# Two matrix products one quarter later in a hand-written order, and three small operations moved from VectorE to ScalarE

## The chip, the cores and the metric

The kernel runs on one core of one Trainium2 chip. The metric is the device time of one execution in microseconds (us). The core's engines are TensorE (PE in the views, PEld for its weight loads), VectorE (DVE), ScalarE (ACT), GpSimd (POOL) and SyncE (SP, which issues DMAs here). They run on their own and meet at semaphores.

## The reference

Sixteen images of 128 channels and 32 x 32 pixels go through three layers (cut to what matters):

```python
# L0: attention over 1024 pixels, 4 heads of 32 channels, per image b
qkv = einsum('oc,bchw->bohw', qkv_w, batchnorm(x)) + qkv_b
attn = softmax(einsum('bnchw,bncyx->bnhwyx', q, k) / sqrt(C))
x = x + out_w @ einsum('bnhwyx,bncyx->bnchw', attn, v) + out_b
# L1: linear attention on t = tokens of x, 8 heads of 16 channels
z = layernorm(t)                      # per token
d = z - mean_of_each_head(z);  u = d / (std_of_each_head(d) + EPS)
k = kln_weight * u + kln_bias;  v = vln_weight * u + vln_bias
t = t + z + z @ (k.T @ v / N)         # per head; k.T @ v comes from u.T @ u
# FFN: 8 experts, the two likeliest of each token
z2 = layernorm(t);  probs = softmax(z2 @ gate_w + gate_b)
t = t + sum over the top 2 experts of probs * (gelu(z2 @ W1 + b1) @ W2 + b2)
```

## The kernel before, in words

One loop of 19 iterations (`FIRST` = -1 to `LAST` = 17) holds a software pipeline over images. In iteration i, TensorE computes the attention of image i, and beside it what comes before and after for its neighbours: q, k, v of image i+1, the first layer norm, `z`, `u` and the Gram product of image i-1, the second layer norm and the gate of image i-2, the expert slots of image i-3. Fourteen images are routed: their tokens are scattered to DRAM by expert and go through the experts in tiles of 256 tokens, from iteration 16 on and after the loop. The last two go through all experts.

An iteration has 32 quarters (q). Each engine walks them in order in its own program, and the tables `AT` (iterations -1 to 15) and `AFTER` (16 and 17) say in which quarter each piece of side work stands. Nothing but semaphores ties the quarters of one engine to those of another. In TensorE's program every even quarter begins with `scores` (L1755, L1758: the scores of one key block, four heads), every odd one with `values` (L1789: probabilities times v); both kinds then have two row tiles (L1814: scores again, by rows, from which VectorE takes the row maxima of the next half image, L1345). Two row tiles have two banks, so a row tile waits until the tile before the last has been reduced. The side products, called pieces, stand between the two row tiles. They all write one PSUM bank (`shared_ps`), so a piece waits until the one before it in the order has been copied out:

```python
def order(pair, p):
    return sorted(LAG, key=lambda n: table(pair, p)[n])   # equal quarters: as in LAG
...
def free_shared(name, pair, p):                           # TensorE, ahead of each piece
    prev_name, prev_pair, prev_p = previous(name, pair, p)
...
    elif prev_name[:4] == "mrow":
        pe.wait_ge(mrow_ready, 2 * b + int(prev_name[4]) + 1)
...
    elif prev_name == "gram":
        pe.wait_ge(gram_out, 3 * b + 2)
```

`LAG` names `mrow0` ahead of `gram` and `usum`.

The pieces that the change is about: **gram** (L1639, 16 passes over `u` of image i-1: u.T @ u and the sum of u), which waits for `u_ready` of GpSimd; **usum** (L1644, the product behind it: it spreads the sum of u over the partitions), which waits for `udiag` that ScalarE makes from gram's result; **mrow0** (L1616: turns the negative row maxima `negm` of image i+1 into a row, which `scores` of the next iteration add), which waits for `negm` of VectorE (`row_maxima`, L1138 to L1147, in q28 behind the first row maximum of that quarter). ScalarE copies gram out (L865 to L869) and mrow0 (L834). In an even quarter its program has a piece between the two exponentials (L928) of that quarter, in an odd one behind them.

`u` is made in a chain over four engines: ScalarE writes `z` (L902); VectorE sums groups of 16 (`gsum`, L1404) and scales the sums to means (L1408); GpSimd subtracts (`d16`, L782); ScalarE squares (L974); VectorE sums the squares (L1412); ScalarE takes logarithm and exponential (L894, L896); VectorE makes the reciprocal deviations (`head_deviations`, up to L1199); GpSimd multiplies (`u`, L787).

For the routed images VectorE also makes slot numbers (`slot_numbers`): it advances the token numbers by 1024 (L1329), sums two products to slot numbers (L1330) and converts these to integers (L1332), which GpSimd's scatter (L715) reads.

Of the kernel before, what the change touches and what calls it, by code (L numbers as in the profile page):

```python
# [10 lines left out]
ALU = mybir.AluOpType  # L11
# [8 lines left out]
def conv_attention_hybrid_kernel(  # L20
# [62 lines left out]
    out_v = out.rearrange("b c h w -> b c (h w)")  # L83


    AT = {'q0': 2, 'k0': 3, 'q1': 4, 'k1': 7, 'rank': 1, 't2_0': 8, 't2_1': 10, 'proj0': 11, 'proj1': 12, 'mrow1': 14, 'v0': 13, 'v1': 16, 'z2T0': 17, 'z2T1': 18, 'logits': 20, 'zT0': 23, 'zT1': 27, 'mrow0': 29, 'gram': 28, 'usum': 30, 'xn': 0, 'values1': 0, 'values0': 17, 'x_bias': 27, 'ln1': 11, 'z2': (12, 14, 14, 15), 'gexp': 21, 'ln0': 16, 'z': (18, 18, 20, 21), 'square': 21, 'ln_heads': 26, 'split': (2, 3, 5, 6), 'norm1': 5, 'norm0': 29, 'd16': (20, 20), 'u': (22, 23), 'scatter': (8, 10, 11, 13, 16, 17, 22, 24), 'max1': 12, 'max0': 28, 'kv1': 2, 'kv2': 4, 'kv3': 5, 'slot_numbers': 4, 'stats1a': 8, 'stats1b': 10, 'deviations1': 11, 'gate': (20, 21, 23, 23, 24, 25, 25, 25, 26, 26, 26, 27, 27, 27, 27, 27), 'prefix': (27, 28, 30), 'stats0a': 11, 'stats0b': 12, 'deviations0': 17, 'gsum': (19, 20), 'ss': (22, 24), 'heads': 26, 'turn': 1, 'den_sum': 2, 'sum': (5, 9, 13, 19), 'den1': 5, 'den0': 21}

    LAG = {
# [3 lines left out]
    }  # L92
    AFTER = (
        {**AT, **{'rank': 0, 't2_0': 10, 't2_1': 10, 'proj0': 10, 'proj1': 12, 'z2T0': 17, 'z2T1': 18, 'logits': 20, 'zT0': 21, 'zT1': 24, 'gram': 28, 'usum': 31, 'values1': 12, 'ln1': 3, 'z2': (12, 13, 14, 14), 'gexp': 19, 'ln0': 15, 'z': (17, 17, 18, 18), 'square': 20, 'ln_heads': 23, 'norm1': 8, 'd16': (19, 20), 'u': (25, 26), 'scatter': (3, 3, 4, 5, 5, 6, 7, 10), 'kv1': 2, 'kv2': 4, 'kv3': 7, 'slot_numbers': 1, 'stats1a': 10, 'stats1b': 10, 'deviations1': 11, 'gate': (23, 23, 24, 24, 25, 25, 26, 27, 27, 28, 28, 29, 29, 29, 29, 30), 'prefix': (26, 28, 29), 'stats0a': 11, 'stats0b': 13, 'deviations0': 16, 'gsum': (18, 19), 'ss': (21, 22), 'heads': 24, 'den1': 3}},
        {**AT, **{'rank': 0, 't2_0': 7, 't2_1': 10, 'proj0': 11, 'proj1': 13, 'z2T0': 17, 'z2T1': 18, 'logits': 20, 'zT0': 21, 'zT1': 23, 'gram': 28, 'usum': 30, 'values1': 4, 'ln1': 11, 'z2': (12, 13, 14, 14), 'gexp': 20, 'ln0': 15, 'z': (17, 17, 18, 18), 'square': 20, 'ln_heads': 23, 'norm1': 5, 'd16': (18, 19), 'u': (25, 26), 'scatter': (0, 0, 2, 5, 8, 11, 14, 17), 'kv1': 0, 'kv2': 4, 'kv3': 6, 'slot_numbers': 0, 'stats1a': 9, 'stats1b': 11, 'deviations1': 11, 'gate': (21, 21, 22, 23, 23, 24, 25, 25, 25, 26, 26, 27, 27, 27, 27, 28), 'prefix': (26, 28, 29), 'stats0a': 11, 'stats0b': 13, 'deviations0': 16, 'gsum': (18, 19), 'ss': (21, 22), 'heads': 24, 'den1': 5}},
    )
    PAIRS, SUM_PARTS = 4, 4
    SUMMED = (0, 1, 2, 3)
# [130 lines left out]
    with ctx:  # L229
# [3 lines left out]
        def sem(name):  # L233
            return ctx.enter_context(nc.semaphore(name))
# [422 lines left out]
        def _(pool):  # L657
# [87 lines left out]
            def iteration(pair, p):  # L745
                at = table(pair, p)
                for q in range(QUARTERS):
                    s, j = divmod(q, 4)
                    for i in SUMMED:
                        for half in (0, 1):  # L750
                            when = 16 * half + at["sum"][i]
                            lag = -(when // QUARTERS)
                            if q == when % QUARTERS and in_range(lag, pair, p):
                                b = image(lag, pair, p)[0]
                                if i in summed_at(2 * b + half):
                                    sum_pair(b, half, i)
                    if in_range(1, pair, p):
                        b, _, par = image(1, pair, p)
                        if q == at["split"][0]:

                            _, prp, parp = image(0, pair, p)
                            if positive(prp + 1):
                                for h in range(NH):
                                    pool.wait_ge(stacked1[parp][h], 16 * STACK1_DMAS * (prp + 1))
                        for c in range(4):
                            if q == at["split"][c]:
                                split(b, par, c)
                    if in_range(-3, pair, p):
                        b, _, par = image(-3, pair, p)
                        for i in range(8):  # L770
                            if q == at["scatter"][i]:
                                scatter(b, par, range(2 * i, 2 * i + 2))
                    if in_range(-1, pair, p):
                        b, _, _ = image(-1, pair, p)
                        if q == at["norm1"]:
                            norm(b, 1)
                        for half in (0, 1):
                            blocks = slice(4 * half, 4 * half + 4)
                            if q == at["d16"][half]:

                                pool.wait_ge(gsum_ready, 4 * b + 2 * half + 2)
                                g.tensor_tensor(grouped(d16[:, blocks, :]), grouped(z[:, blocks, :]),  # L782
                                                wide16(gsum[:, 1, :])[:, blocks], ALU.subtract).then_inc(d_ready, 1)
                            if q == at["u"][half]:

                                pool.wait_ge(rs_step, 5 * b + 5)
                                g.tensor_tensor(grouped(u[:, blocks, 0:C]), grouped(d16[:, blocks, :]),  # L787
                                                wide16(rs16[:, 1, :])[:, blocks], ALU.mult).then_inc(u_ready, 1)
                    if q == at["norm0"] and in_range(0, pair, p):
                        norm(image(0, pair, p)[0], 0)  # L790
                    for t in steps_at(q, pair, p):
                        scatter_y(t - 3)
# [21 lines left out]
        def _(act):  # L814
# [98 lines left out]
            def iteration(pair, p):  # L913
                at = table(pair, p)
                for q in range(QUARTERS):
# [153 lines left out]
        def _(dve):  # L1069
# [256 lines left out]

            def slot_numbers(b, par):
                dve.wait_ge(slot_step, 4 * b + 3)
                v.tensor_scalar(token[:, :], token[:, :], float(N), None, ALU.add).then_inc(token_ready, 1)  # L1329
                v.tensor_reduce(slot_of[:, :, :], slot[:, 1:3, :, :], AX.X, ALU.add).then_inc(slot_step, 1)  # L1330
                dve.wait_ge(slot_step, 4 * b + 4)
                v.tensor_copy(slot_idx[:, par, :], slot_of[:, :, :].rearrange("p c k -> p (c k)")).then_inc(idx_ready, 1)  # L1332

            def iteration(pair, p):
                at = table(pair, p)
                for q in range(QUARTERS):
# [53 lines left out]
                    if in_range(-1, pair, p):  # L1390
# [7 lines left out]
                        for half in (0, 1):  # L1398
                            blocks = slice(4 * half, 4 * half + 4)
                            groups = slice(4 * NG * half, 4 * NG * half + 4 * NG)  # L1400
                            if q == at["gsum"][half]:
# [611 lines left out]
```

## Time and profile before

| what | value |
|---|---|
| runs | 1842.6, 1842.03 and 1848.09 us (median 1842.6) |
| profiled execution | first to last instruction 1848.0 us, which goes with the run of 1848.09 us: about 0.1 us lies around the span |
| TensorE busy | 1707.3 us, 92% of the span |
| VectorE, ScalarE, GpSimd busy | 72%, 62%, 69% |
| mean granted clock of TensorE | 0.964 |

The span has three parts: a start of some 50 us, the image loop to about 1390 us, and expert tiles with the sums and stores to the end. In the loop an iteration takes some 84 us. A granted clock of 1.00 is TensorE at 2.4 GHz, 0.5 is 1.2 GHz; a stretch that holds both shows a value between.

### The profile page before, as it was taken

The numbers are of one execution on the slowest core, as the hardware profiler recorded it, in microseconds if no ns is written. First come the engines' busy times: TensorE is split into PE (matmuls) and PEld (weight loads), VectorE is DVE, ScalarE is ACT, GpSimd is POOL, SyncE is SP. The second block draws the span as 40 slices with busy tenths as digits, with TensorE's granted clock in tenths as the row PEclk, the third lists the DMA queues.
The fourth block names the chain that finished last, engine by engine and source line by source line (L and its number), as shares of the span: only waits on it lengthen the run. The fifth ranks groups of instructions, "written<-read, shape, count | busy, mean of one in ns | idle before, by whom it ended". The sixth has DMA issues, their size and how long they took to land. (4 is left out here: it accounts for less than half of the span.)

```text
span 1848.0 us, 36083 instructions
## 1 busy us (share of the span) xinstructions
PE 1707.3 (92%) x11741; PEld 842.7 (46%) x11741; DVE 1338.6 (72%) x3555; ACT 1140.8 (62%) x2019; POOL 1279.6 (69%) x1165
## 2 busy tenths in 40 slices
PE   5999989999999999999999999999976889999999
PEld 2223333333434333333334343333335778888776
DVE  5567788888878888888878888878755555555474
ACT  2556565666656665666666566656544777777553
POOL 1466747787878778787778787787874767777500
PEclk8899999999999999999999999999997889999998
DMA  2302112130303031230303030312212334454394
GB/s 77 91 13 58 35 47 61 46 90 29 88 19 88 19 92 46 65 85 23 92 27 89 19 89 18 92 37 63 67 58 78 92 95 127 156 173 137 102 288 157
DMA packets 119206, 144.43 MB, mean 78 GB/s; under 512 B 18248, under 2 KB 83044, under 8 KB 119024
## 3 DMA queue, kind: packets, MB, share of 16 engines
q1 hardware_dynamic: 103856, 110.91, 21.4%
q0 software_dynamic: 14784, 31.23, 5.0%
q8 instruction: 97, 1.59, 0.4%
q14 instruction: 85, 0.70, 0.1%
q10 hardware_dynamic: 384, 0.00, 0.0%
HBM read 59.38 MB, written 50.05 MB: 59 GB/s over the span
## 5 line engine op out<-in xcount | busy, mean ns | idle before, releaser
L1345 DVE TENSOR_REDUCE rowmax<-psum 128x1 f32<-128x512 f32 x992 | 652.3, 682 | 210.0 <-PE psum L1814 203.9
L1814 PE MATMUL psum<-arena 128*128 128x512 bf16 x992 | 360.4, 390 | 38.2 <-DVE rowmax L1345 35.7
L928 ACT ACTIVATE arena<-psum 128x1024 f32<-128x1024 f32 x256 | 253.9, 1022 | 161.1 <-PE psum L1758 161.1
L928 ACT ACTIVATE probs<-psum 128x1024 f32<-128x1024 f32 x256 | 253.1, 1020 | 114.5 <-PE psum L1758 114.2
L1755 PE MATMUL psum<-qk 32*128 32x512 f32 x2048 | 293.9, 643 | 10.0 <-ACT probs L928 4.6
L1814 PEld LDWEIGHTS psum<-arena 128*128 128x128 bf16 x992 | 88.5, 99 | 448.0 <-DVE rowmax L1345 333.4
L715 POOL DMA_INDIRECT sorted_scratch<-rows,slot_idx x224 | 220.3, 984 | 96.8 <-issue 51.9
L729 POOL TENSOR_TENSOR probs<-probs 128x512 f32<-128x512 f32 x172 | 218.9, 1273 | 27.2 <-PE psum L1789 16.1
L729 POOL TENSOR_TENSOR arena<-arena 128x512 f32<-128x512 f32 x172 | 218.9, 1272 | 22.0 <-PE psum L1789 10.1
L803 POOL DMA_INDIRECT y_scratch<-xn,d_tile x120 | 116.9, 974 | 57.5 <-issue 28.7
L1865 PE MATMUL psum<-qk 128*128 128x256 f32 x476 | 129.5, 396 | 20.0 <-ACT qk L988 18.9
L803 POOL DMA_INDIRECT y_scratch<-qk,d_tile x118 | 115.0, 974 | 45.9 <-issue 26.0
L706 POOL TENSOR_TENSOR part<-qk,part 128x512 bf16<-128x512 f32 x64 | 74.0, 1157 | 94.3 <-ACT qk L848 90.7
L1789 PE MATMUL psum<-arena,v_sb 128*32 128x512 f32 x1024 | 138.5, 613 | 0.0
L1789 PE MATMUL psum<-probs,v_sb 128*32 128x512 f32 x1024 | 136.4, 605 | 0.0
L1755 PEld LDWEIGHTS psum<-qk 32*128 32x128 f32 x2048 | 80.5, 183 | 120.5 <-issue 78.3
L1882 PEld LDWEIGHTS psum<-arena,x_in 128*128 128x128 f32 x952 | 128.0, 198 | 13.8 <-issue 7.5
L1882 PE MATMUL psum<-arena,x_in 128*128 x952 | 130.9, 282 | 3.1 <-ACT x_in L1000 3.1
L1000 ACT ACTIVATE x_in<-psum,b_tile 128x256 f32<-128x256 f32 x238 | 100.0, 472 | 38.4 <-issue 31.8
L729 POOL TENSOR_TENSOR arena<-arena,probs 128x512 f32<-128x512 f32 x80 | 102.1, 1277 | 12.9 <-PE psum L1789 7.6
L729 POOL TENSOR_TENSOR probs<-probs,arena 128x512 f32<-128x512 f32 x80 | 102.0, 1275 | 5.5
L1758 PE MATMUL psum<-mrow,ones_b 2*128 2x512 bf16 x1024 | 102.0, 378 | 0.0
(256 smaller groups left out, 2876.5 us busy)
## 6 DMA issues: line engine op xcount, KB each, us to landing
arena<-part SPq DMA_DIRECT2D x256, 128.0 KB, 3.1
part<-sorted_scratch SPq DMA_DIRECT2D x119, 144.0 KB
x_in<-in_x_dram SPq DMA_DIRECT2D x16, 512.0 KB, 3.2
x_res<-in_x_dram SPq DMA_DIRECT2D x16, 512.0 KB, 5.7
t_scratch<-t SPq DMA_DIRECT2D x14, 512.0 KB, 6.4
arena<-t_scratch SPq DMA_DIRECT2D x10, 512.0 KB
probs<-y_scratch SPq DMA_DIRECT2D x16, 256.0 KB, 4.2
out_dram<-v_sb SPq DMA_DIRECT2D x16, 256.0 KB, 3.9
```

Source lines behind the costliest of these rows:

```text
L715: g.indirect_dma_start(out=sorted_dram, out_offset=bass.IndirectOffsetOnAxis(ap=slot_idx[:, par, n:n + 1], axis=0), in_=rows[:, par, n % B ...
L729: piece = g.tensor_tensor(even[:, cols], even[:, cols], odd[:, cols], ALU.add)
L803: g.indirect_dma_start(out=y_dram, out_offset=bass.IndirectOffsetOnAxis(ap=d_tile[:, i, k:k + 1], axis=0), in_=y_out[i][:, k, :], in_offse ...
L928: a.activation(group[:, 2 * i:2 * i + 2, :].rearrange("p s n -> p (s n)"), st_pair[i], ACT.Exp, scale=float(C) ** -0.5).then_inc(exp_done, 1)
L1000: a.activation(hid[t % 2][:, j, :], bank[t % 2][:, j * TILE:(j + 1) * TILE], ACT.Gelu, bias=b1_tile[:, t % 2, j:j + 1]).then_inc(hid_ready, 1)
L1345: v.tensor_reduce(rowmax[:, half, kh, h, j:j + 1], row_ps[kh][:, :], AX.X, ALU.max)\
L1755: t_.matmul(st_ps[h], qk[rows_, par, 1, keys], qk[rows_, par, 0, queries], start=True, stop=False)
L1758: last = t_.matmul(st_ps[h], ones_b[rows_, :], mrow[rows_, half, :], start=False, stop=True)
L1789: mm = t_.matmul(av_ps[rows_, :], v_sb[:, par, kb, rows_], group[:, h, :], start=(kb == 0), stop=(kb == NKB - 1))
L1814: t_.matmul(ps[:, :], qs1[:, par, h, qb * P:(qb + 1) * P], ks1[:, par, h, kh * HALF:(kh + 1) * HALF], start=True, stop=True)\
L1865: last = t_.matmul(bank[t % 2][:, j * TILE:(j + 1) * TILE], w1_tile[t % 2][:, j * P:(j + 1) * P], zT_tile[t % 2], start=True, stop=True)
L1882: last = t_.matmul(bank[4 + t % 2][:, k * P:(k + 1) * P], hid[t % 2][:, j, k * P:(k + 1) * P], w2[:, bass.ds(e, 1), j, :].rearrange("p a c ...
```

## The change

Four edits. (1) In `AT`, gram stands in q29 in place of q28 and usum in q31 in place of q30; the tables `AFTER` keep theirs. mrow0 stays in q29, and at equal quarters `LAG` puts it ahead, so it now comes before gram. (2) The scaling of the group sums moves from VectorE to ScalarE, as an activation (Copy with a scale) with a place of its own, `gmean`, in q19 and q21; GpSimd's `d16` waits for it. (3) The conversion of the slot numbers and (4) the advance of the token numbers move to ScalarE (`slot_indices`, in the quarter of `slot_numbers`, behind a wait for VectorE's sum). VectorE's next slot sum waits until ScalarE has read the last one.

```diff
-    AT = {... 'mrow0': 29, 'gram': 28, 'usum': 30, ... 'gsum': (19, 20), ...}
+    AT = {... 'mrow0': 29, 'gram': 29, 'usum': 31, ... 'gsum': (19, 20), 'gmean': (19, 21), ...}
...
 # GpSimd, iteration
                             if q == at["d16"][half]:
-                                pool.wait_ge(gsum_ready, 4 * b + 2 * half + 2)
+                                pool.wait_ge(gmean_ready, 2 * b + half + 1)
...
 # ScalarE, iteration
+                        for half in (0, 1):
+                            groups = slice(4 * NG * half, 4 * NG * half + 4 * NG)
+                            if q == at["gmean"][half]:
+                                act.wait_ge(gsum_ready, 2 * b + half + 1)
+                                a.activation(gsum[:, 1, groups], gsum[:, 0, groups], ACT.Copy, scale=1.0 / G16)\
+                                 .then_inc(gmean_ready, 1)
...
+                    if q == at["slot_numbers"] and in_range(-3, pair, p):
+                        b, _, par = image(-3, pair, p)
+                        slot_indices(b, par)
...
+            def slot_indices(b, par):
+                act.wait_ge(slot_step, 4 * b + 4)
+                a.activation(slot_idx[:, par, :], slot_of[:, :, :].rearrange("p c k -> p (c k)"), ACT.Copy)\
+                 .then_inc(idx_ready, 1)
+                a.activation(token[:, :], token[:, :], ACT.Copy, bias=float(N)).then_inc(token_ready, 1)
...
 # VectorE
             def slot_numbers(b, par):
                 dve.wait_ge(slot_step, 4 * b + 3)
-                v.tensor_scalar(token[:, :], token[:, :], float(N), None, ALU.add).then_inc(token_ready, 1)
+                if positive(b):
+                    dve.wait_ge(idx_ready, b)
                 v.tensor_reduce(slot_of[:, :, :], slot[:, 1:3, :, :], AX.X, ALU.add).then_inc(slot_step, 1)
-                dve.wait_ge(slot_step, 4 * b + 4)
-                v.tensor_copy(slot_idx[:, par, :], slot_of[:, :, :].rearrange("p c k -> p (c k)")).then_inc(idx_ready, 1)
...
-                                dve.wait_ge(gsum_ready, 4 * b + 2 * half + 1)
-                                v.tensor_scalar(gsum[:, 1, groups], gsum[:, 0, groups], 1.0 / G16, None, ALU.mult)\
-                                 .then_inc(gsum_ready, 1)
```

TensorE's program in q28 to q30 of iteration 14 before, from the first row tile of q28 to the scores of q30, with the semaphores that each row waits for (L1639 is gram, L1616 mrow0):

```order
L1814 MATMUL psum<-arena 128x512 [waits row_used]
L1639 MATMUL psum<-u 128x129 [waits zT_ready,u_ready]
L1639 MATMUL psum<-u 128x129 x7
L1814 MATMUL psum<-arena 128x512 [waits row_used]
L1789 MATMUL psum<-arena,v_sb 32x512 [waits exp_done]
L1789 MATMUL psum<-arena,v_sb 32x512 x3
L1814 MATMUL psum<-arena 128x512 [waits row_used]
L1616 MATMUL psum<-identb,negm 128x128 [waits gram_out,negm_ready]
L1616 MATMUL psum<-identb,negm 128x128 x3
L1814 MATMUL psum<-arena 128x512 [waits row_used]
L1755 MATMUL psum<-qk 128x512 [waits exp_done]
```

The same stretch of the changed kernel, whose lines are numbered 14 higher there (L1653 is gram, L1630 mrow0):

```order
L1828 MATMUL psum<-arena 128x512 [waits row_used] x2
L1803 MATMUL psum<-arena,v_sb 32x512 [waits exp_done]
L1803 MATMUL psum<-arena,v_sb 32x512 x3
L1828 MATMUL psum<-arena 128x512 [waits row_used]
L1630 MATMUL psum<-identb,negm 128x128 [waits zT_ready,negm_ready]
L1630 MATMUL psum<-identb,negm 128x128 x3
L1653 MATMUL psum<-u 128x129 [waits mrow_ready,u_ready]
L1653 MATMUL psum<-u 128x129 x7
L1828 MATMUL psum<-arena 128x512 [waits row_used]
L1769 MATMUL psum<-qk 128x512 [waits exp_done]
```

Gram has moved behind the values, a row tile and mrow0, and directly behind mrow0; in place of `zT_ready` it waits for `mrow_ready`, ScalarE's copy of mrow0, and mrow0 no longer waits for `gram_out`.

ScalarE's program in q27 to q30 of iteration 11 before, from the biasing of the residual in q27 on (L928 are exponentials, L865 to L869 copy gram out, L834 mrow0):

```order
L949 ACTIVATE x_res<-x_res,bo 128x1024
L928 ACTIVATE probs<-psum 128x1024
L865 ACTIVATE usum_sb<-psum 128x1
L866 ACTIVATE kvw<-psum,kcol 128x128
L868 ACTIVATE udiag<-ident,usum_sb 128x128
L869 ACTIVATE kcc<-usum_sb,kb_n,kcol 128x1
L928 ACTIVATE probs<-psum 128x1024
L834 ACTIVATE mrow<-psum 128x512
```

And in the changed kernel:

```order
L950 ACTIVATE x_res<-x_res,bo 128x1024
L929 ACTIVATE probs<-psum 128x1024 x2
L835 ACTIVATE mrow<-psum 128x512
L866 ACTIVATE usum_sb<-psum 128x1
L867 ACTIVATE kvw<-psum,kcol 128x128
L869 ACTIVATE udiag<-ident,usum_sb 128x128
L870 ACTIVATE kcc<-usum_sb,kb_n,kcol 128x1
```

Both exponentials of q28 now stand ahead of gram's copies, and mrow0's copy ahead of them too.

## Rows read from the trace of the kernel before

**Rows 1.** The page's first part: busy us, share of the span, instructions.

```profile
PE 1707.3 (92%) x11741; PEld 842.7 (46%) x11741; DVE 1338.6 (72%) x3555; ACT 1140.8 (62%) x2019; POOL 1279.6 (69%) x1165
```

**Rows 2.** Waits of TensorE, whole span: us in total, times, longest.

```profile
PE psum L1814 <- DVE rowmax L1345: 35.7, 69, 1.7
PE psum L1639 <- POOL u L787: 20.3, 15, 2.8
```

**Rows 3.** Windows, gram (L1639) alone, two of 14: stretch, length, PE busy, granted clock.

```profile
1036.50:1040.30 3.80, 3.33 (x16) 0.62 0.12 39
1121.00:1124.50 3.50, 2.05 (x16) 1.00 0.13 42
```

**Rows 4.** Timeline of TensorE, iteration 12: start, length, what, [idle before <-releaser].

```profile
1119.71 0.39 PE L1814 MATMUL psum<-arena 128*128 128x512 bf16 x1 [0.86 <-DVE rowmax L1345]
1121.34 2.05 PE L1639 MATMUL psum<-u 128*128 128x129 f32 x16 [1.24 <-POOL u L787]
1123.23 0.38 PE L1814 MATMUL psum<-arena 128*128 128x512 bf16 x1
1123.54 1.06 PE L1789 MATMUL psum<-arena,v_sb 128*32 128x512 f32 x8
...
1124.77 0.39 PE L1616 MATMUL psum<-identb,negm 128*128 128x128 bf16 x4
...
1125.39 1.14 PE L1755 MATMUL psum<-qk 32*128 32x512 f32 x8
```

**Rows 5.** Timeline of VectorE in the same stretch.

```profile
1119.02 1.22 DVE L1345 TENSOR_REDUCE rowmax<-psum 128x1 f32<-128x512 f32 x2
...
1122.02 0.68 DVE L1345 TENSOR_REDUCE rowmax<-psum 128x1 f32<-128x512 f32 x1
...
1123.05 0.23 DVE L1147 SCALAR_TENSOR_TENSOR negm<-rowm,negm 128x16 bf16<-128x16 f32 x1
```

**Rows 6.** Timelines of GpSimd and of ScalarE in the same stretch.

```profile
1119.19 2.09 POOL L787 TENSOR_TENSOR u<-d,rs 128x512 f32<-128x512 f32 x2 [4.67 <-DVE rs L1199]
...
1125.22 0.60 ACT L834 ACTIVATE mrow<-psum 128x512 bf16<-128x512 f32 x1
```

**Rows 7.** Timeline of TensorE, iteration 11: row tile of q28, scores of q30.

```profile
1035.21 0.39 PE L1814 MATMUL psum<-arena 128*128 128x512 bf16 x1 [0.86 <-DVE rowmax L1345]
...
1042.39 1.14 PE L1755 MATMUL psum<-qk 32*128 32x512 f32 x8
```

**Rows 8.** Groups of VectorE and ScalarE (busy us, mean ns), and L1408's min/median/max.

```profile
L1408 DVE TENSOR_SCALAR gsum<-gsum 128x32 f32<-128x32 f32 x32 | 31.7, 990 | 1.1
L1332 DVE CAST slot_idx<-slot_of 128x16 uint32<-128x16 f32 x14 | 15.0, 1070 | 0.5
L896 ACT ACTIVATE ss<-ss 128x64 f32<-128x64 f32 x16 | 4.1, 256 | 0.5
L1408 DVE TENSOR_SCALAR gsum<-gsum x32: 181/853/1728, 170.6 to 1424.3; 128x32 f32<-128x32 f32 x32
```

**Rows 9.** Timelines of VectorE, ScalarE and TensorE in iterations 10 and 11.

```profile
890.36 0.69 DVE L1345 TENSOR_REDUCE rowmax<-psum 128x1 f32<-128x512 f32 x1 [0.72 <-PE psum L1814]
...
1022.28 0.69 DVE L1345 TENSOR_REDUCE rowmax<-psum 128x1 f32<-128x512 f32 x1 [1.42 <-PE psum L1814]
...
1013.06 1.94 ACT L928 ACTIVATE probs<-psum 128x1024 f32<-128x1024 f32 x2
1021.70 1.06 ACT L974 ACTIVATE u<-d 128x1024 f32<-128x1024 f32 x1 [3.75 <-POOL d L782]
...
1020.56 1.14 PE L1755 MATMUL psum<-qk 32*128 32x512 f32 x8
```

**Rows 10.** Timeline of TensorE at the end of the last attention (iteration 15) and behind.

```profile
1368.56 3.64 PE L1639 MATMUL psum<-u 128*128 128x129 f32 x16 [2.82 <-POOL u L787]
...
1374.19 1.14 PE L1755 MATMUL psum<-qk 32*128 32x512 f32 x8 [1.00 <-ACT probs L928]
...
1376.90 0.43 PE L1664 MATMUL psum<-chosen,tri 128*128 128x64 f32 x2
```

More of the change, by code:

```diff
@@ L83, in conv_attention_hybrid_kernel @@
     out_v = out.rearrange("b c h w -> b c (h w)")
-    AT = {'q0': 2, 'k0': 3, 'q1': 4, 'k1': 7, 'rank': 1, 't2_0': 8, 't2_1': 10, 'proj0': 11, 'proj1': 12, 'mrow1': 14, 'v0': 13, 'v1': 16, 'z2T0': 17, 'z2T1': 18, 'logits': 20, 'zT0': 23, 'zT1': 27, 'mrow0': 29, 'gram': 28, 'usum': 30, 'xn': 0, 'values1': 0, 'values0': 17, 'x_bias': 27, 'ln1': 11, 'z2': (12, 14, 14, 15), 'gexp': 21, 'ln0': 16, 'z': (18, 18, 20, 21), 'square': 21, 'ln_heads': 26, 'split': (2, 3, 5, 6), 'norm1': 5, 'norm0': 29, 'd16': (20, 20), 'u': (22, 23), 'scatter': (8, 10, 11, 13, 16, 17, 22, 24), 'max1': 12, 'max0': 28, 'kv1': 2, 'kv2': 4, 'kv3': 5, 'slot_numbers': 4, 'stats1a': 8, 'stats1b': 10, 'deviations1': 11, 'gate': (20, 21, 23, 23, 24, 25, 25, 25, 26, 26, 26, 27, 27, 27, 27, 27), 'prefix': (27, 28, 30), 'stats0a': 11, 'stats0b': 12, 'deviations0': 17, 'gsum': (19, 20), 'ss': (22, 24), 'heads': 26, 'turn': 1, 'den_sum': 2, 'sum': (5, 9, 13, 19), 'den1': 5, 'den0': 21}
+    AT = {'q0': 2, 'k0': 3, 'q1': 4, 'k1': 7, 'rank': 1, 't2_0': 8, 't2_1': 10, 'proj0': 11, 'proj1': 12, 'mrow1': 14, 'v0': 13, 'v1': 16, 'z2T0': 17, 'z2T1': 18, 'logits': 20, 'zT0': 23, 'zT1': 27, 'mrow0': 29, 'gram': 29, 'usum': 31, 'xn': 0, 'values1': 0, 'values0': 17, 'x_bias': 27, 'ln1': 11, 'z2': (12, 14, 14, 15), 'gexp': 21, 'ln0': 16, 'z': (18, 18, 20, 21), 'square': 21, 'ln_heads': 26, 'split': (2, 3, 5, 6), 'norm1': 5, 'norm0': 29, 'd16': (20, 20), 'u': (22, 23), 'scatter': (8, 10, 11, 13, 16, 17, 22, 24), 'max1': 12, 'max0': 28, 'kv1': 2, 'kv2': 4, 'kv3': 5, 'slot_numbers': 4, 'stats1a': 8, 'stats1b': 10, 'deviations1': 11, 'gate': (20, 21, 23, 23, 24, 25, 25, 25, 26, 26, 26, 27, 27, 27, 27, 27), 'prefix': (27, 28, 30), 'stats0a': 11, 'stats0b': 12, 'deviations0': 17, 'gsum': (19, 20), 'gmean': (19, 21), 'ss': (22, 24), 'heads': 26, 'turn': 1, 'den_sum': 2, 'sum': (5, 9, 13, 19), 'den1': 5, 'den0': 21}
     LAG = {
@@ L93, in conv_attention_hybrid_kernel @@
     AFTER = (
-        {**AT, **{'rank': 0, 't2_0': 10, 't2_1': 10, 'proj0': 10, 'proj1': 12, 'z2T0': 17, 'z2T1': 18, 'logits': 20, 'zT0': 21, 'zT1': 24, 'gram': 28, 'usum': 31, 'values1': 12, 'ln1': 3, 'z2': (12, 13, 14, 14), 'gexp': 19, 'ln0': 15, 'z': (17, 17, 18, 18), 'square': 20, 'ln_heads': 23, 'norm1': 8, 'd16': (19, 20), 'u': (25, 26), 'scatter': (3, 3, 4, 5, 5, 6, 7, 10), 'kv1': 2, 'kv2': 4, 'kv3': 7, 'slot_numbers': 1, 'stats1a': 10, 'stats1b': 10, 'deviations1': 11, 'gate': (23, 23, 24, 24, 25, 25, 26, 27, 27, 28, 28, 29, 29, 29, 29, 30), 'prefix': (26, 28, 29), 'stats0a': 11, 'stats0b': 13, 'deviations0': 16, 'gsum': (18, 19), 'ss': (21, 22), 'heads': 24, 'den1': 3}},
@@ L95, in conv_attention_hybrid_kernel @@
-        {**AT, **{'rank': 0, 't2_0': 7, 't2_1': 10, 'proj0': 11, 'proj1': 13, 'z2T0': 17, 'z2T1': 18, 'logits': 20, 'zT0': 21, 'zT1': 23, 'gram': 28, 'usum': 30, 'values1': 4, 'ln1': 11, 'z2': (12, 13, 14, 14), 'gexp': 20, 'ln0': 15, 'z': (17, 17, 18, 18), 'square': 20, 'ln_heads': 23, 'norm1': 5, 'd16': (18, 19), 'u': (25, 26), 'scatter': (0, 0, 2, 5, 8, 11, 14, 17), 'kv1': 0, 'kv2': 4, 'kv3': 6, 'slot_numbers': 0, 'stats1a': 9, 'stats1b': 11, 'deviations1': 11, 'gate': (21, 21, 22, 23, 23, 24, 25, 25, 25, 26, 26, 27, 27, 27, 27, 28), 'prefix': (26, 28, 29), 'stats0a': 11, 'stats0b': 13, 'deviations0': 16, 'gsum': (18, 19), 'ss': (21, 22), 'heads': 24, 'den1': 5}},
+        {**AT, **{'rank': 0, 't2_0': 10, 't2_1': 10, 'proj0': 10, 'proj1': 12, 'z2T0': 17, 'z2T1': 18, 'logits': 20, 'zT0': 21, 'zT1': 24, 'gram': 28, 'usum': 31, 'values1': 12, 'ln1': 3, 'z2': (12, 13, 14, 14), 'gexp': 19, 'ln0': 15, 'z': (17, 17, 18, 18), 'square': 20, 'ln_heads': 23, 'norm1': 8, 'd16': (19, 20), 'u': (25, 26), 'scatter': (3, 3, 4, 5, 5, 6, 7, 10), 'kv1': 2, 'kv2': 4, 'kv3': 7, 'slot_numbers': 1, 'stats1a': 10, 'stats1b': 10, 'deviations1': 11, 'gate': (23, 23, 24, 24, 25, 25, 26, 27, 27, 28, 28, 29, 29, 29, 29, 30), 'prefix': (26, 28, 29), 'stats0a': 11, 'stats0b': 13, 'deviations0': 16, 'gsum': (18, 19), 'gmean': (18, 19), 'ss': (21, 22), 'heads': 24, 'den1': 3}},
@@ new lines, in conv_attention_hybrid_kernel @@
+        {**AT, **{'rank': 0, 't2_0': 7, 't2_1': 10, 'proj0': 11, 'proj1': 13, 'z2T0': 17, 'z2T1': 18, 'logits': 20, 'zT0': 21, 'zT1': 23, 'gram': 28, 'usum': 30, 'values1': 4, 'ln1': 11, 'z2': (12, 13, 14, 14), 'gexp': 20, 'ln0': 15, 'z': (17, 17, 18, 18), 'square': 20, 'ln_heads': 23, 'norm1': 5, 'd16': (18, 19), 'u': (25, 26), 'scatter': (0, 0, 2, 5, 8, 11, 14, 17), 'kv1': 0, 'kv2': 4, 'kv3': 6, 'slot_numbers': 0, 'stats1a': 9, 'stats1b': 11, 'deviations1': 11, 'gate': (21, 21, 22, 23, 23, 24, 25, 25, 25, 26, 26, 27, 27, 27, 27, 28), 'prefix': (26, 28, 29), 'stats0a': 11, 'stats0b': 13, 'deviations0': 16, 'gsum': (18, 19), 'gmean': (18, 19), 'ss': (21, 22), 'heads': 24, 'den1': 5}},
```

1 line of the change is left out of this document (added).

## Prediction

> **What bounds the kernel now.** I read the page's first part: TensorE is busy for 92% of the span, the others for 61 to 73% [rows 1]. So the order of work in TensorE's program sets the end, and a change is worth what it adds to or takes from TensorE's waits, plus what the clock does. Then the waits of TensorE [rows 2]. Two of them touch the change: row tiles wait for VectorE's row maxima 69 times, 35.7 us in all, and gram waits for GpSimd's u 15 times, 20.3 us in all. That u-wait is what a later gram could win back, so I looked at gram alone, iteration by iteration [rows 3]. In the fourteen iterations that also hold mrow0 it took 2.05 us at a granted clock of 1.00 (four of them) or 3.0 to 3.7 us with the clock at half for part of it (ten of them). Last, the timelines of TensorE, VectorE, GpSimd and ScalarE in the same stretch of iteration 12, one of the four at full clock [rows 4 to 6]: there the whole change can be replayed.
>
> What happens there now: the first row tile of q28 runs at 1119.71. Gram is next. GpSimd ends u at 1121.28 (1119.19 + 2.09), gram starts 0.06 later, at 1121.34, and runs for 2.05. Row tile (1123.23), values (1123.54), a row tile, mrow0 (1124.77), scores of q30 (1125.39). Meanwhile VectorE, busy with the gate's small steps after 1120.24, takes the row maximum of q28 from 1122.02 to 1122.70 and ends negm at 1123.28 (1123.05 + 0.23) [rows 5]. mrow0 needs that negm and waits for it nowhere, because gram fills TensorE's time until then.
>
> **Gram and usum a quarter later.** I replay the new order with the same rows. u and negm keep their times, since both hang on VectorE's work ahead, which the move leaves as it is. A start lags its releaser by 0.06, as gram's does.
> - The second row tile of q28 needs the reduction that ends at 1120.24 (1119.02 + 1.22): it starts at 1120.30 in place of 1123.23.
> - The values follow by 0.31 (1123.54 − 1123.23): 1120.61, ending near 1121.7.
> - The row tile of q29 needs the bank that VectorE's row maximum frees at 1122.70: 1122.76. A new wait of about 1.1.
> - mrow0 needs negm at 1123.28: 1123.34, and takes 0.39: 1123.73. In front of it TensorE has only that one row tile.
> - Gram stands directly behind mrow0 and uses the same bank, so it waits for ScalarE's copy: 0.06 + 0.60 [rows 6], 1124.39. Gram starts at 1124.45. u has been there since 1121.28.
> - Row tile 1.89 behind gram's start (1123.23 − 1121.34): 1126.34. Scores of q30 0.31 later: 1126.65.
>
> Before, these scores ran at 1125.39: **+1.26 us for each of 14 iterations, +17.6 us.** The u-wait of 1.24 is gone, but two waits that gram covered, for VectorE (1.1 and 0.2) and for ScalarE's copy (0.7), now lie open, because gram is moved behind the one step that it hid. Behind the waiting gram stand the second row tile of q29 and the scores of q30; behind ScalarE's wait for mrow0 stand gram's copies and the exponentials of q30, whose scores come later anyway. usum stands two quarters behind gram as before, so it adds nothing. Lower bound: were neither VectorE's bank nor negm late, mrow0 would start 1.23 behind the values (1124.77 − 1123.54), at 1121.84, its copy would end at 1122.89 and gram start at 1122.95; with the 2.20 from gram to the scores, 1125.15: −0.24, or −3.4 us in 14. I take the replay, as each of its steps is a row.
>
> **The clock.** In iteration 11 gram ran at 0.62 [rows 3], and from q28's first row tile to the scores it was 7.18 us (1035.21 to 1042.39) against 5.68 in iteration 12 (1119.71 to 1125.39) [rows 4, 7]: a fall costs 1.5 us. Each came with a wait of TensorE ahead (0.86 and then the one for u). After the change TensorE idles some 3.1 us in this stretch (0.9, 0.2, 1.1, 0.2 and 0.7), against 2.1 before (0.9 and 1.2), but in smaller pieces between which it works. No row shows what that does. Bounds: none falls, 10 × 1.5 = −15.0; all fourteen fall, 4 × 1.5 = +6.0. I take the same ten of fourteen, 0: more idle time speaks for more falls, its shorter pieces for fewer.
>
> **The end of attention.** Iteration 15 has gram but no mrow0 [rows 10]. Before, gram waits 2.82 for u, and the scores of the last quarter wait a further 1.00 for exponentials that stand behind gram's copies on ScalarE. After, values run in the 2.82 and the second half of the exponentials goes ahead of the copies: scores right behind gram, near 1372.2 (1368.56 + 3.64) instead of 1374.19. That is 2.0 at most, and 0 if usum's wait for the copies takes it back; I take **−1.5**.
>
> **Three operations from VectorE to ScalarE.** VectorE loses 31.7 us of scaling and 15.0 us of conversion [rows 8], and 14 adds no longer than the conversions' 1.07. But right behind both places it waits for TensorE: 0.72 in q4 (890.36) and 1.42 in q20 (1022.28) [rows 9]. What it saves ends in those waits, and the replay's stretch is not moved. ScalarE gains 32 scalings and 28 slot operations, at some 0.26 us each (an activation of 128x64 takes 256 ns). It idles 3.75 ahead of the square [rows 9], which is the chain that the scaling belongs to. The one price: the exponentials of q20 wait behind the scaling for VectorE's sum, by up to 1.0; those ahead end at 1015.00 and the scores of q22 come at 1020.56, so 5.5 us cover it. Without that cover each would cost up to 1.0, 14 us in all. Below, at most what the first rival gives. I take 0.
>
> Here the trace has something to weigh. The scaling of one and the same shape took 181 ns at least and 1728 at most [rows 8]: VectorE is being held up by something. The Trainium skill ("SBUF — State Buffer", section "SBUF: two separate sides") has VectorE and GpSimd share one pair of ports, locked for a whole instruction, and ScalarE on its own; the spread agrees, and by that rule the move takes these hold-ups off VectorE, which is the first rival below.
>
> **Sum.** +17.6 − 1.5 + 0 + 0 = +16.1. The profiled execution takes 1848.1 and would take 1864.2; it is 5.5 above the median of the runs, and the median goes from 1842.6 to **1858.7**.
>
> **Rivals.**
> - *VectorE's freed time reaches the row tiles* (the other side). The 31.7 + 15.0 us and the hold-ups leave VectorE; the 35.7 us that row tiles wait for it vanish: +16.1 − 35.7 = −19.6, 1823.0. For it: mean 990 ns against 181 at least. Against: VectorE waits for TensorE behind each place. It decides once more than 16.1 / 35.7 = 45% of those waits go. Chance 0.10.
> - *The waits vanish and nothing takes their place.* If negm came as early as u, the wait for u (1.24 × 14 = 17.4), the falls (15.0) and the 1.5 would go: −33.9, 1808.7. Against: negm's end at 1123.28 is worked out from a row [rows 5]. Chance 0.05.
> - *The falls vanish.* The idle time is cut in pieces and the clock holds: 16.1 − 15.0 = +1.1, 1843.7, no change. For: iteration 12 kept its clock through waits of 0.86 and 1.24. Chance 0.15.
> - *All fourteen fall.* 16.1 + 6.0 = +22.1, 1864.7. Chance 0.08.
> - *ScalarE's new waits hold the scores*, as with no cover above: 16.1 + 14 = +30.1, 1872.7. Chance 0.04.
>
> **How the numbers follow.** My forecast has 0.58. A change of this kernel can be told from none from about 0.3%, 5.5 us. Faster: 0.10 + 0.05 = 0.15. Same: 0.15. Slower: 0.58 + 0.08 + 0.04 = 0.70. The range goes from 1838 (the lower bound of the move, −3.4 − 1.5, which also takes in the case without falls) to 1867 (all fall, and 2 above it, for what the bounds of the end of attention leave); outside lie the two faster rivals and the last, 0.19. The forecast's own range, with three falls more or less, is 1854 to 1863.
>
> **What would show it.** Right: gram's idle time is put down to ScalarE's mrow in place of GpSimd's u, near 0.7 each; the first row tile of q29 waits about 1.1 for VectorE; at full clock the scores of q30 come some 6.9 us after q28's first row tile (5.7 before); VectorE's busy time falls by 47 us or more, and its waits for TensorE rise by as much. Wrong: row tiles elsewhere wait clearly less than 35.7 us in all (first rival); gram at 1.00 in nearly all iterations (third) or in none (fourth); scores of q22 that wait for exponentials (fifth); mrow0 that doesn't wait for negm, if VectorE got to it sooner than replayed.

## The result, and the profile after

The changed kernel takes 1868.0 us (median of 4 runs, 1861.8 to 1871.6) where the kernel before takes 1843.6: ratio 1.0116, 95% interval 1.0088 to 1.0145. Run again later beside 13 runs of the kernel before it took 1865.6, ratio 1.0105 (1.0083 to 1.0127). By these ratios (the first is not the quotient of its two medians, which would be 1.0132) it is slower by 19 to 21 us; +16.1 was forecast. The first median lies 1.0 above the end of the range, 1867; the second lies within it, as do both ratios applied to the forecast's 1842.6 (1862 to 1864). The profiled execution's span went from 1848.0 to 1867.2 us, by 19.2.

The page's first part, busy us and share of the span by engine:

```profile
PE 1709.5 (92%) x11741; PEld 841.6 (45%) x11741; DVE 1287.5 (69%) x3495; ACT 1148.1 (61%) x2079; POOL 1279.9 (69%) x1165
```

VectorE (DVE) is 51 us less busy than before [rows 1], ScalarE only 7 us more, and TensorE's busy time has grown by 2 us: some 17 of the 19 us are idle time of TensorE. Its waits (total, times, longest), to be read against [rows 2]:

```profile
PE psum L1828 <- DVE rowmax L1362: 54.3, 92, 3.1
...
PE psum L1653 <- ACT mrow L835: 10.9, 14, 0.8
...
PE psum L1630 <- DVE negm L1164: 5.7, 14, 2.0
...
PE psum L1653 <- POOL u L788: 1.8, 1, 1.8
```

The wait for GpSimd's u is gone but for 1.8 of its 20.3 us: the change did what it says. In its place stand 18.6 us more of row tiles that wait for row maxima, 10.9 us of gram waiting for ScalarE's copy of mrow0, and 5.7 us of mrow0 waiting for negm. Where that happens is seen in TensorE's timeline of iteration 10, one of the four that keep the clock up (start, length, what, [idle before <-releaser]); it answers to [rows 4]:

```profile
968.07 0.39 PE L1828 MATMUL psum<-arena 128*128 128x512 bf16 x1 [0.85 <-DVE rowmax L1362]
968.67 0.39 PE L1828 MATMUL psum<-arena 128*128 128x512 bf16 x1 [0.20 <-DVE rowmax L1362]
968.99 1.07 PE L1803 MATMUL psum<-arena,v_sb 128*32 128x512 f32 x8
971.12 0.39 PE L1828 MATMUL psum<-arena 128*128 128x512 bf16 x1 [1.07 <-DVE rowmax L1362]
971.70 0.40 PE L1630 MATMUL psum<-identb,negm 128*128 128x128 bf16 x4 [0.19 <-DVE negm L1164]
972.88 2.02 PE L1653 MATMUL psum<-u 128*128 128x129 f32 x16 [0.78 <-ACT mrow L835]
...
975.05 1.14 PE L1769 MATMUL psum<-qk 32*128 32x512 f32 x8
```

From the first row tile to the scores it is 6.98 us (975.05 − 968.07), against 5.68 in [rows 4]. VectorE in the same stretch works at the times that [rows 5] gave, only moved with the iteration: its row maximum of q28 comes 2.99 behind the pair, negm 4.02 behind it (3.00 and 4.03 before).

```profile
967.39 1.22 DVE L1362 TENSOR_REDUCE rowmax<-psum 128x1 f32<-128x512 f32 x2
...
970.38 0.68 DVE L1362 TENSOR_REDUCE rowmax<-psum 128x1 f32<-128x512 f32 x1
...
971.41 0.23 DVE L1164 SCALAR_TENSOR_TENSOR negm<-rowm,negm 128x16 bf16<-128x16 f32 x1
```

Gram alone, in windows (stretch, length, PE busy, PEld busy, granted clock), iterations 9 and 10 of the fourteen that hold mrow0; ten lie below 1.00 and four at it, as many as before [rows 3]:

```profile
884.90:888.70 3.80, 3.65 (x16) 3.38 (x16) 0.55 0.02 7
972.80:975.00 2.20, 2.02 (x16) 1.86 (x16) 1.00 0.05 12
```

Iteration 2 cost more than any other. TensorE first, then VectorE, then GpSimd, there:

```profile
281.83 0.61 PE L1828 MATMUL psum<-arena 128*128 128x512 bf16 x1 [3.08 <-DVE rowmax L1362]
283.80 0.61 PE L1630 MATMUL psum<-identb,negm 128*128 128x128 bf16 x4 [1.36 <-DVE negm L1164]
```

```profile
278.51 1.19 DVE L1306 TENSOR_TENSOR chosen<-lg 128x64 f32<-128x64 f32 x1
279.74 1.30 DVE L1308 TENSOR_TENSOR rows<-lg,chosen 128x64 f32<-128x64 f32 x1
...
281.10 0.68 DVE L1362 TENSOR_REDUCE rowmax<-psum 128x1 f32<-128x512 f32 x1
```

```profile
276.32 2.07 POOL L788 TENSOR_TENSOR u<-d,rs 128x512 f32<-128x512 f32 x2 [10.12 <-DVE rs L1216]
278.35 10.68 POOL L730 TENSOR_TENSOR probs<-probs,arena 128x512 f32<-128x512 f32 x8
```

`chosen` and `rows` are two of the gate's small steps ahead of q28's row maximum. They take 1.19 and 1.30 here and 0.29 and 0.22 in iteration 10. In iteration 2 no image is routed yet, so GpSimd has no scatters behind u and begins its sums of probabilities at once; in iteration 10 two scatters stand between. So the row maximum and negm come later, the two waits sum to 4.4 us in place of 1.3, and nothing covers them.

In iteration 1 there is no gate yet, and the steps that make negm meet the sums themselves: mrow0 waits 2.02 for negm. VectorE there:

```profile
191.27 1.21 DVE L1162 TENSOR_SCALAR negm<-rowm 128x16 bf16<-128x16 f32 x1
192.52 1.33 DVE L1164 SCALAR_TENSOR_TENSOR negm<-rowm,negm 128x16 bf16<-128x16 f32 x1
```

In iteration 10 these two take 0.20 and 0.23.

The end of attention, which answers to [rows 10]:

```profile
1392.16 2.05 PE L1653 MATMUL psum<-u 128*128 128x129 f32 x16 [1.82 <-POOL u L788]
1394.14 1.14 PE L1769 MATMUL psum<-qk 32*128 32x512 f32 x8
...
1397.45 0.41 PE L1678 MATMUL psum<-chosen,tri 128*128 128x64 f32 x2 [0.54 <-DVE kvw L1250]
```

The values run ahead of gram, the scores follow it with no wait for exponentials, and rank comes 5.29 us behind gram's start (8.34 before). Of these 3.05 us, 1.6 is gram at full clock (2.05 against 3.64), so 1.5 is the order.

### The profile page after: what moved, and what is told of

It is laid out like the page before. It is cut to its first block and busy times, and to the rows that moved or that the text cites. A ratio compares the mean times of both kernels' runs of the same rounds, so it can differ in the third digit from the quotient of the medians.

```text
span 1867.2 us, 36096 instructions
## 1 busy us (share of the span) xinstructions
PE 1709.5 (92%) x11741; PEld 841.6 (45%) x11741; DVE 1287.5 (69%) x3495; ACT 1148.1 (61%) x2079; POOL 1279.9 (69%) x1165
## 5 line engine op out<-in xcount | busy, mean ns | idle before, releaser
L730 POOL TENSOR_TENSOR probs<-probs 128x512 f32<-128x512 f32 x172 | 219.1, 1274 | 27.3 <-PE psum L1803 16.1
```

What stands on the lines that cost most here:

```text
L730: piece = g.tensor_tensor(even[:, cols], even[:, cols], odd[:, cols], ALU.add)
```

## The experiments

Two theories stood first. Lost cover: gram hid TensorE's wait for negm, and behind mrow0 it hides nothing. Rival: the three operations on ScalarE, or its longer queue, cost the time. All ratios are to the kernel before on the same chip, with 95% intervals. Edits are in `AT` unless said.

**Gram and usum alone**, on the kernel before.

```diff
-'gram': 28, 'usum': 30
+'gram': 29, 'usum': 31
```

> The kernel before with gram in q29 and usum in q31 alone; the three small operations stay on VectorE. Lost cover (gram filled TensorE's time until negm, and now stands behind negm's product and its copy): nearly the whole loss is here, +17 to +26 us, ratio 1.009 to 1.014, with gram's wait put down to ScalarE's copy of mrow0 (0.8 each) and the first row tile of q29 waiting 1.1 for VectorE. Rival, that ScalarE's new waits or its longer queue cost the time: under +5 us here, ratio below 1.003.

1863.2 us, 1.0091 (1.0075 to 1.0106), with the wait for ScalarE's copy as large as in the changed kernel (its waits of TensorE):

```profile
PE psum L1639 <- ACT mrow L834: 10.9, 14, 0.8
```

The loss is at the lower end of what lost cover expected (some 17 us), and far above the rival's 5. The move is the loss.

**The three operations alone**: the changed kernel with gram back in q28 and usum in q30.

```diff
-'gram': 29, 'usum': 31
+'gram': 28, 'usum': 30
```

> The changed kernel with gram back in q28 and usum in q30, so only the three small operations have moved. Lost cover: no difference, ratio 0.997 to 1.003, while VectorE is busy some 50 us less and waits as much longer for TensorE. Rival, ScalarE's new waits: +15 us or more, ratio 1.008 and up. Second rival, that VectorE's freed time reaches the row tiles: their 35.7 us of waits shrink and the ratio is below 0.995.

1846.7 us, 1.0001 (0.9988 to 1.0014). VectorE is busy 1282.2 us, 56 less than before, and nothing comes of it; ScalarE's instructions take 13.4 us for what took VectorE 56 (the 31.7 and 15.0 of [rows 8], and 9.3 for the advance). The groups, busy us and mean ns:

```profile
L977 ACT ACTIVATE gsum<-gsum 128x32 f32<-128x32 f32 x32 | 7.3, 229 | 23.7 <-DVE gsum L1421 23.7
L993 ACT ACTIVATE slot_idx<-slot_of 128x16 uint32<-128x16 f32 x14 | 3.1, 223 | 1.9 <-DVE slot_of L1349 1.9
L995 ACT ACTIVATE token<-token 128x8 f32<-128x8 f32 x14 | 3.0, 212 | 0.0
```

Both the ScalarE rival and the first rival of the prediction fall.

**The changed kernel once more**, unaltered.

> The changed kernel once more, beside the others on one chip. If the move of gram and usum is all of its loss, it agrees with the kernel that has that move alone: ratio to before 1.008 to 1.011. Rival, that the three operations on ScalarE add to it once gram stands late: 1.012 or more.

1.0105 (1.0083 to 1.0127), which holds the 1.0091 of the move alone. The two parts add up; the 0.0014 between them, some 3 us, lies within the intervals, so a cost of a few us for the three operations beside a late gram is not excluded.

**An early negm**: the changed kernel, with the gate's last five steps and the first two prefix steps one quarter later.

```diff
-'gate': (..., 27, 27, 27, 27, 27), 'prefix': (27, 28, 30)
+'gate': (..., 28, 28, 28, 28, 28), 'prefix': (28, 29, 30)
```

> The changed kernel with the gate's last five steps and the prefix steps one quarter later on VectorE, so that the row maximum and negm of q28 come some 1.5 us earlier. Lost cover through a late negm: the waits of q29's row tile (1.1 in iteration 12) and of mrow0 go, gram starts about 1.1 earlier, the scores of q30 come 0.1 before those of the kernel before; ratio to before 0.996 to 1.001, and iteration 2 loses its extra 4 us. Rival, that ScalarE's copy ahead of gram or the clock's falls are the cost: gram still waits 0.8 for the copy, the loss stays above +11 us, ratio 1.006 and up.

1839.3 us, 0.9964 (0.9952 to 0.9976). TensorE in iteration 12, and one line of iteration 2:

```profile
1114.36 0.39 PE L1828 MATMUL psum<-arena 128*128 128x512 bf16 x1 [0.85 <-DVE rowmax L1362]
1114.95 0.39 PE L1828 MATMUL psum<-arena 128*128 128x512 bf16 x1 [0.20 <-DVE rowmax L1362]
...
1116.27 0.39 PE L1828 MATMUL psum<-arena 128*128 128x512 bf16 x1
1116.51 0.40 PE L1630 MATMUL psum<-identb,negm 128*128 128x128 bf16 x4
1117.68 2.02 PE L1653 MATMUL psum<-u 128*128 128x129 f32 x16 [0.78 <-ACT mrow L835]
1119.86 1.14 PE L1769 MATMUL psum<-qk 32*128 32x512 f32 x8
```

```profile
280.92 0.40 PE L1630 MATMUL psum<-identb,negm 128*128 128x128 bf16 x4 [2.02 <-DVE negm L1164]
```

In iterations 3 to 14 the waits of 1.07 and 0.19 are gone, the wait for the copy stands, and the scores come 5.50 behind the first row tile (5.68 before, 6.98 in the changed kernel), all at full clock. So the late negm was the loss there, as lost cover has it, and the rival (the copy) isn't. In iterations 1 and 2 mrow0 still waits 2.02 for negm, whose steps meet GpSimd's sums: from q28's scores to the next iteration the two take 7.4 us more than before (9.1 in the changed kernel), so the expectation that iteration 2 loses its extra 4 us held only in part. That the whole became faster than the kernel before comes mostly from the clock: gram's clock fell in 2 of the 14 iterations, these two, not in 10.

**Gram first**: the changed kernel with mrow0 behind gram, and the kernel before with the same order (gram in q29, usum in q31, mrow0 in q30), its three operations left on VectorE.

```diff
-'mrow0': 29
+'mrow0': 30
```

> The changed kernel with mrow0 in q30, so gram comes first in q29; VectorE's gate steps stay where they were. Lost cover: gram again fills the time until negm, with nothing of ScalarE's in front of it; row tile of q29 still waits 1.1, gram starts near 1.73 after the values' end, scores of q30 within 0.15 of the kernel before, mrow0 costs 0.25 more in q30: ratio 0.996 to 1.002, lower by 0.008 if the clock stays up. Rival, that gram in q29 is itself too late: 1.006 or more, as in the changed kernel.

> The kernel before with gram in q29, usum in q31 and mrow0 in q30; the three operations stay on VectorE and the gate's steps where they were. If ScalarE's part is worth nothing, as with gram first and ScalarE's operations: ratio 0.992 to 0.996, with no clock fall at gram and the full-clock length of the stretch as before. Rival, that it takes VectorE's freed time as well: 0.998 or more.

0.9938 (0.9918 to 0.9958) and 0.9929 (0.9908 to 0.9950). The second, TensorE in iteration 12, and its granted clock over the stretch (the number behind the busy times):

```profile
1108.48 0.39 PE L1814 MATMUL psum<-arena 128*128 128x512 bf16 x1 [0.85 <-DVE rowmax L1345]
1109.07 0.39 PE L1814 MATMUL psum<-arena 128*128 128x512 bf16 x1 [0.20 <-DVE rowmax L1345]
...
1111.53 0.39 PE L1814 MATMUL psum<-arena 128*128 128x512 bf16 x1 [1.07 <-DVE rowmax L1345]
1111.76 1.95 PE L1639 MATMUL psum<-u 128*128 128x129 f32 x16
...
1113.85 1.14 PE L1755 MATMUL psum<-qk 32*128 32x512 f32 x8
```

```profile
1105.00:1120.00 15.00, 12.79 (x98) 5.57 (x98) 13.99 (x33) 8.51 (x15) 11.16 (x10) 1.00 0.04 11
```

Gram again fills the time until negm and itself waits for nothing. At full clock nothing is won by the start of the next iteration: the scores of q30 come 5.37 behind the row tile (0.31 earlier than before), and q30 then holds mrow0 and is 0.38 longer. The gain is the clock, which falls near gram in one iteration (the second, where a row tile waits 3.08 for VectorE) instead of ten, and the end of attention.

**Late gate with gram in q28**: the kernel before with the three operations on ScalarE, and the gate edit above.

> The kernel before with the three operations on ScalarE and the gate's last five steps and prefix one quarter later, gram still in q28. Lost cover: an early negm is worth nothing here, since gram waits for u as before (20 us in all) and covers negm anyway; clock falls as before; ratio 0.998 to 1.002. Rival, that the gate's place alone makes the gain of the kernel with the late gate: ratio 0.990 to 0.997.

1905.4 us, 1.0315 (1.0293 to 1.0336): 58 us more than before, where neither theory had a loss above 4. VectorE and GpSimd in iteration 14:

```profile
1344.19 0.69 DVE L1362 TENSOR_REDUCE rowmax<-psum 128x1 f32<-128x512 f32 x1 [1.83 <-PE psum L1828]
1344.79 0.88 DVE L1300 TENSOR_TENSOR lg<-lg,rank_w 128x64 f32<-128x64 f32 x1
1345.71 0.22 DVE L1302 TENSOR_REDUCE lred<-lg 128x8 f32<-128x64 f32 x1
1345.96 1.05 DVE L1304 TENSOR_TENSOR lg<-lg,lred 128x64 f32<-128x64 f32 x1
1347.04 1.31 DVE L1306 TENSOR_TENSOR chosen<-lg 128x64 f32<-128x64 f32 x1
1348.39 1.31 DVE L1308 TENSOR_TENSOR rows<-lg,chosen 128x64 f32<-128x64 f32 x1
```

```profile
1343.30 0.97 POOL L716 DMA_INDIRECT sorted_scratch<-rows,slot_idx  x1 [0.30 <-issue]
1344.28 10.73 POOL L730 TENSOR_TENSOR probs<-probs,arena 128x512 f32<-128x512 f32 x8
```

With gram in q28, the second row tile of q28 comes only behind it, VectorE waits 1.83 for that tile, and its steps then fall beside GpSimd's sums: those with two inputs in SBUF take 0.9 to 1.3 us, the reduction with one stays at 0.22. A row tile of q30 waits 3.2 for them, and TensorE's clock falls behind that wait (the values of q31 take 1.93 us, 1.06 at full clock). It is the mechanism of iteration 2, now in iterations 2 to 14: from the scores of q30 to the next iteration each takes 8.2 to 8.4 us in place of 3.6.

**Late gate and gram first**, on the changed kernel and on the kernel before.

> The changed kernel with mrow0 behind gram (q30) and the gate's last five steps and prefix one quarter later. Lost cover: nothing stands between the values and gram but a row tile whose bank is free; u has been there for 0.7 us. Scores of q30 some 0.9 earlier than in the kernel before: 14 times 0.9 and the gain at the end of attention, -13 to -17 us, ratio about 0.992; if the clock no longer falls in these pieces, 10 times 1.5 more, ratio 0.983. Rival, that VectorE is merely late elsewhere: its delayed gate steps hold the row tiles of q29 and q30, and the ratio is 0.998 to 1.004.

> The kernel before with gram in q29, mrow0 in q30, usum in q31 and the late gate, the three operations on VectorE. If ScalarE's part is worth nothing even where VectorE is busy to the end of the stretch: 0.992 to 0.996, as with ScalarE's operations. Rival, that VectorE without its freed time comes later to the late gate steps: 0.998 or more.

0.9938 (0.9920 to 0.9955) and 0.9935 (0.9914 to 0.9957): no better than gram first alone, and the same with and without ScalarE's three operations. Gram ran at full clock in all fourteen iterations of both, and for that case the first expectation had 0.983: it missed by some 20 us. VectorE and TensorE in iteration 12 of the first:

```profile
1111.41 1.81 DVE L1308 TENSOR_TENSOR rows<-lg,chosen 128x64 f32<-128x64 f32 x1
```

```profile
1114.01 0.39 PE L1828 MATMUL psum<-arena 128*128 128x512 bf16 x1 [0.59 <-DVE rowmax L1362]
```

The scores of q30 come 1.46 earlier than before at full clock, but q30 and q31 then take 4.62 us in place of 3.58: mrow0 stands there, and a row tile waits 0.59 for row maxima behind `rows`, which takes 1.81 beside the sums. Iteration 2 takes over 3 us more than before. What is left against gram first, 0.47 in most iterations, is too little for the intervals.

**Where the steps land**: the late gate with gram first, its last five steps spread further, or three more of them moved, or only `rows` moved.

```diff
 # spread
-'gate': (..., 26, 26, 26, 27, 27, 27, 27, 27), 'prefix': (27, 28, 30)
+'gate': (..., 26, 26, 26, 28, 28, 29, 29, 31), 'prefix': (29, 30, 30)
 # three more
+'gate': (..., 28, 28, 28, 29, 29, 30, 30, 31), 'prefix': (30, 31, 31)
 # only rows
+'gate': (..., 26, 26, 26, 28, 28, 28, 28, 31), 'prefix': (28, 29, 30)
```

> As the kernel with gram first and a late gate, but its last five steps spread over q28, q29 and q31, so that VectorE's longest small step (1.8 us for the rows beside GpSimd's sums) no longer stands before the row maxima of q29. The row tile of q30 there waited 0.6: that goes, 14 times 0.6 = 8 us, ratio to before 0.988 to 0.991. Rival, that the next row tile waits in its place: ratio 0.993 to 0.995, unchanged against that kernel.

> As the kernel with the spread gate, with three more steps moved behind the row maxima of q28 and the rest a quarter further on. The first row tile of q28 waits 0.9 for VectorE in the kernel before and gram's u hangs on the same queue: 0.7 us of steps taken from ahead of it, 14 times up to 0.7 = 10 us, ratio 0.983 to 0.988. Rival, that rank at the start of the next iteration now waits for the late prefix: ratio 0.990 or more, with a wait of rank for VectorE.

> As gram first with the late gate, but the gate's last step (rows, 1.8 us beside GpSimd's sums, 0.2 to 0.3 beside its scatters) alone in q31. If VectorE's small steps are slow only beside GpSimd's sums, the wait of 0.6 at the row tile of q30 goes: ratio 0.987 to 0.991. Rival, that another small step meets the sums in its place (four_of or before, or rows itself in q31): 0.993 to 1.000.

1.0011 (0.9998 to 1.0024), 1.0087 (1.0066 to 1.0108) and 0.9945 (0.9924 to 0.9967). All three expectations failed: the first two took a step to cost the same wherever it stands, and in the third its rival came true (with `rows` gone, `two_of` takes 1.80 in its place, and the row tile of q30 still waits 0.45). `chosen` (min/median/max ns over its 16) in the changed kernel and in the spread one:

```profile
L1306 DVE TENSOR_TENSOR chosen<-lg x16: 225/298/1190, 278.5 to 1561.9; 128x64 f32<-128x64 f32 x16
```

```profile
L1306 DVE TENSOR_TENSOR chosen<-lg x16: 224/1302/1306, 283.0 to 1542.3; 128x64 f32<-128x64 f32 x16
```

In the spread kernel TensorE then waits for row maxima in q31, ahead of usum (L1658), up to 1.6 us and twelve times:

```profile
PE psum L1658 <- DVE rowmax L1362: 19.3, 12, 1.6
```

With three more steps moved the first row tile of the next iteration waits 1.9 for row maxima behind the gate's leftovers, and the clock falls there. Moving `rows` alone gave no gain that its interval tells from gram first.

## Why the prediction was right

- **What bounds, and where.** TensorE's order in q28 to q30 and VectorE's negm, as read. The replay gave idle times of 0.9, 0.2, 1.1, 0.2 and 0.7 in the stretch; measured were 0.85, 0.20, 1.07, 0.19 and 0.78, with the releasers forecast.
- **+1.26 for each of 14.** At equal clock the stretch is 1.30 longer in iteration 10 than in [rows 4]. From q28's scores to the next iteration, iterations 3 to 14 together take 14.3 us more (15.1 forecast; the clock fell near gram in eight of them, in nine before). The term was mis-sized in iterations 1 and 2, where 2.5 was forecast and 9.1 measured (3.54 and 5.51; 5.5 of it more idle time, the rest the clock): I took iteration 12 for all fourteen, though the first two have no scatters on GpSimd that keep its sums away from VectorE's small steps. Before, gram hid that too, but for 0.4 in iteration 2.
- **The clock.** I took ten falls of fourteen, and ten there were. No row stood behind that choice, and the count came out by luck: iteration 1 fell that had not, one fewer of iterations 3 to 14 did, and in iteration 2 gram ran at 1.2 GHz from end to end (3.78 us), more than a fall of 1.5 covers.
- **The end of attention.** −1.5 forecast; −3.0 measured to rank (−3.7 to the scores of q30), half of it a fall that did not come. So the order is worth the 1.5, and the fall was not foreseen.
- **The three operations.** 0 forecast; ratio 1.0001 alone. VectorE lost 51 to 56 us of work, and its freed time ended in waits: in the kernel with the three operations alone its row maxima wait 207.4 us for row tiles and 37.3 more whose releaser the trace doesn't name, against 203.9 before. The 14 us named as the price without cover count fourteen iterations, while the scaling stands in the fifteen from 1 to 15; only the last rival's time hangs on it.
- **The sum.** In the profiled execution 14.3 + 9.1 − 3.7 (the last from q28's scores of iteration 15 to those of q30) makes 19.7; the spans differ by 19.2, and the −0.5 between was not followed up. By the ratios the time moved by 19 to 21 against 16.1. So the sum came near the mark partly by luck: the 6.6 that iterations 1 and 2 cost beyond their 2.5 were offset by 0.8 in the others and 2.2 at the end of attention.
- **Two slips without effect.** The 1848.1 taken for the profiled execution doesn't fit: every run whose span is on record took some 1.7 us longer than its span, so a span of 1848.0 goes with some 1849.7, which is none of the three runs listed. And the other engines are busy for 62 to 72% in [rows 1], not 61 to 73%. The forecast of the median uses neither.
- **The rivals.** The first (freed time reaches the row tiles) and the last (ScalarE holds the scores) are refuted by the kernel with the three operations alone. The second, third and fourth did not happen here; the kernels with an early negm or gram first show that the falls can vanish, so the third was a real possibility whose condition this change doesn't meet.

Why the small steps slow down can be read from where they end. They are slow in each kernel where they meet GpSimd's sums (1.34 us each, 10.73 for 8) and fast beside its scatters. In the late gate with gram in q28 the sums begin at 1344.28, so at 1.34 each the first four end at 1345.62, 1346.96, 1348.30 and 1349.65; the four slow steps shown there end at 1345.67, 1347.01, 1348.35 and 1349.70, each 0.05 behind a sum. All 54 executions over 0.5 us of these four lines in that run end within 0.12 us behind one of GpSimd's TENSOR_TENSOR operations. So do the 24 of 32 over 0.5 us of the scaling in the kernel before (181 ns to 1728 in [rows 8]): the step waits until GpSimd's operation is over. The Trainium skill ("SBUF — State Buffer", section "SBUF: two separate sides") gives this as a lock on the port pair that VectorE and GpSimd share: a VectorE operation with two SBUF inputs is shut out while a GpSimd operation that reads SBUF runs. The rows agree, a two-input step with 1.31 and a reduction with 0.22 beside the same sums. Two inputs are not the whole condition here: the scaling and the 1.21 us of negm's L1162 in iteration 1 are steps with one. An experiment with GpSimd's sums elsewhere wasn't run.

The best kernels here take gram and usum a quarter later with mrow0 behind them: 0.993 to 0.995 of the kernel before, with or without ScalarE's part.

## What to carry to other kernels

A wait that looks worth removing may cover another: before a step is moved later, replay the stretch with the same rows and see what its neighbours wait for once it no longer stands there. Replay it in the iterations that differ (the first, the last), not in a typical one alone. And an operation's price goes with its place: a small two-input VectorE step costs 0.22 us or 1.3, by what GpSimd does at the time.

## What the hardware showed that I had not expected

The clock near gram goes with how TensorE's idle time is laid out, and not with its sum alone. In iterations 3 to 14 each of these kernels has the same waits every time. Waits of 0.9 and 1.2 ahead of gram (kernel before) went with 1.2 GHz in part of gram in nine of these twelve, and 0.85, 0.20, 1.07, 0.19 and 0.78 (changed) in eight. With 0.85, 0.20 and 0.78 (early negm), and with 0.85, 0.20 and 1.07 (gram first), it fell in none, though the last sums to the same 2.1 us as before. The falls that those kernels did have near gram came in iterations 1 and 2, behind a wait of 2.02 (early negm) or 3.08 (gram first). The order of the products differs between these kernels too, and no run separates it from the waits: what decides it stays open.
